# Expert feed-forward of a two-block convolution and expert model: units of 384 tokens, blocks of 512 columns, one unrolled order

## The reference

```python
def _L1_ffn_ref(x, Wm, bm, expert_emb, W1, b1, W2, b2, Wo, bo):
    h = x @ Wm + bm
    t = h.reshape(bs * L_ * H, HD)                 # 8 heads of 32
    w = jax.nn.softmax(t @ expert_emb, axis=-1)    # 16 experts
    topw, topi = jax.lax.top_k(w, 2)
    hmid = jax.nn.gelu(jnp.einsum('td,edi->tei', t, W1) + b1, approximate=False)   # 32 -> 128
    eo = jnp.einsum('tei,eio->teo', hmid, W2) + b2                                 # 128 -> 32
    sel = jnp.take_along_axis(eo, topi[:, :, None], axis=1)
    comb = (sel * topw[:, :, None]).sum(axis=1)
    return comb.reshape(bs, L_, d) @ Wo + bo       # added to the token
```

## Time and profile before

| what | value |
|---|---|
| time, median of 3 runs | 3064.53 us (3064.31 to 3074.47) |
| the profiled execution | 3055.83 us, its span 3054.1 us |
| PE busy | 2221.5 us, 73% of the span |
| DVE busy | 1406.6 us, 46% |
| ACT busy | 1319.1 us, 43% |
| POOL busy | 1021.1 us, 33% |
| the expert feed-forward | from about 1990 us to the end |

### The profile page before, as it was taken

One profiled execution on the slowest core, in us unless ns is written; L12 is line 12 of the kernel. 1 busy time (PEld: TensorE's weight loads), 2 busy tenths in 40 slices (PEclk: granted clock), 3 DMA queues, 4 the chain that ended last, 5 costly groups with the idle time before them and its releaser, 6 DMA issues. The chain is left out here.

```text
span 3054.1 us, 47716 instructions
## 1 busy us (share of the span) xinstructions
PE 2221.5 (73%) x13261; PEld 1209.0 (40%) x13262; DVE 1406.6 (46%) x2065; ACT 1319.1 (43%) x1759; POOL 1021.1 (33%) x796
## 2 busy tenths in 40 slices
PE   3999289999576740008755558489999999999998
PEld 1444155555343520006642225244444444444444
DVE  3565233333334566002225545456665556666553
ACT  1443111111133530002111114278788888888887
POOL 4332211110000001760027610056555555555554
PEclk7999657777687875559986669799999999999999
DMA  1010121110001633535542202265566565556554
GB/s 30 27 27 6 42 58 41 42 47 22 4 1 60 224 113 101 155 113 166 172 132 69 64 27 71 74 150 134 127 139 140 132 138 127 127 131 147 127 132 101
DMA packets 236895, 285.57 MB, mean 94 GB/s; under 512 B 29172, under 2 KB 218052, under 8 KB 236676
## 3 DMA queue, kind: packets, MB, share of 16 engines
q1 hardware_dynamic: 198116, 232.95, 31.0%
q0 software_dynamic: 12288, 25.72, 2.8%
q10 hardware_dynamic: 26400, 25.70, 2.4%
HBM read 209.00 MB, written 75.25 MB: 93 GB/s over the span
## 5 line engine op out<-in xcount | busy, mean ns | idle before, releaser
L2088 DVE SCALAR_TENSOR_TENSOR BIG<-psMO,b_s,BIG 128x392 f32<-128x392 f32 x512 | 315.1, 622 | 399.3 <-PE psMO L1971 395.2
L1958 POOL TENSOR_TENSOR BIG<-BIG 128x784 f32<-128x784 f32 x192 | 367.5, 1917 | 293.5 <-DVE BIG L2088 286.9
L2011 PE MATMUL ps<-x_r,w_r 128*128 128x392 f32 x1376 | 374.4, 372 | 0.7 <-ACT at L2047 0.5
L2047 ACT ACTIVATE xv<-ps,b_s 128x784 f32<-128x784 f32 x336 | 297.5, 911 | 52.7 <-PE ps L2011 51.9
L2011 PEld LDWEIGHTS ps<-x_r,w_r 128*128 128x128 f32 x1376 | 228.7, 189 | 210.1 <-issue 174.2
L1971 PE MATMUL psMO<-ex,w_s 128*32 128x392 f32 x512 | 213.1, 498 | 51.0 <-DVE BIG L2064 33.0
L1971 PE MATMUL psMO<-xv,w_s 128*32 128x392 f32 x2048 | 223.6, 507 | 23.3 <-issue 8.5
L1404 POOL DMA_INDIRECT gath<-yg_d,idx x128 | 133.6, 1044 | 268.3 <-DVE idx L1415 226.5
L1369 ACT ACTIVATE xv<-ps 128x512 f32<-128x512 f32 x66 | 39.4, 597 | 419.7 <-PE ps L1347 419.7
L1971 PE MATMUL psMO<-rz,w_s 128*32 128x392 f32 x512 | 216.3, 505 | 0.0
L1971 PE MATMUL psMO<-at,w_s 128*32 128x392 f32 x512 | 216.3, 505 | 0.0
(11 more groups left out here) (363 smaller groups left out, 4368.8 us busy)
## 6 DMA issues: line engine op xcount, KB each, us to landing
BIG<-wt_d SPq DMA_DIRECT2D x512, 196.0 KB, 4.1
BIG<-hs_d SPq DMA_DIRECT2D x128, 196.0 KB
xg_d<-zeros SPq DMA_DIRECT2D x64, 264.0 KB
xv<-xg_d SPq DMA_DIRECT2D x66, 256.0 KB, 3.1
BIG<-ypad_d SPq DMA_DIRECT2D x288, 56.0 KB
xv<-x SPq DMA_DIRECT2D x64, 196.0 KB, 3.5
yg_d<-ex ACTq DMA_DIRECT2D x33, 256.0 KB, 3.4
yg_d<-sq ACTq DMA_DIRECT2D x33, 256.0 KB, 3.4
```

Source lines behind the costliest of these rows:

```text
L1958: m = eng.tensor_tensor(dst, dst, src, ALU.add)
L2011: mm = eng.matmul(psA[bufs[m]][:, hh, 0:CH], w1_r[:, group * 4 + e], x_r[:, half, pair * 2 + hh], start=True, stop=True)
L2047: eng.activation(hid[m % 8], psA[bufs[m]][:, :, 0:CH], ACT.Gelu, bias=b1_s[:, ex_:ex_ + 1]).then_inc(Q["gel"], 1)
L2088: eng.scalar_tensor_tensor(out=gsum[:, it % 2, q], in0=psY[hh][:, 0:CH], scalar=b2_s[:, it % 4:it % 4 + 1], in1=wb[:, it % 2, q], op0=ALU. ...
```

## The change

Only the expert feed-forward changes, with the layout of the two device-memory arrays that feed it. The tokens are now cut into 16 pieces of 384 and a rest of 128. A piece is worked as two units `w` of four heads each, and the rest is one unit of eight heads, so that there are NU = 33 units. A unit is 1536 columns (the last 1024), which is three blocks of 512 (two). It has four groups of four experts, so there are 132 groups g.

A first product is now three matmuls of 512 columns with one weight into one of two PSUM buffers of three banks, and a gelu is 1536 columns long. A second product fills one of two banks with 512 columns, three times for a group. The two banks `psY` are now used strictly in turn by everything that needs one, with two counters, `put` (filled by PE) and `got` (emptied by DVE).

Everything is written out in 137 slots k with no loop. Slot k holds the four first products of group k and the second products of group k - 1 after the first product of experts 1, 2 and 3. An extra piece of work, if there is one, stands behind the first product of expert 0: the fold of unit w in slot 4w + 6, the output products of piece c in slots 8c + 11 and 8c + 12, the gate transposes of chunk r in slot 8r - 3. The copies of POOL are gone, since DVE writes the first group's results into `gacc` itself. The hidden tiles, `gacc` and `fin` lie in `BIG`, and the gates and `gsum` have buffers of their own. The router still works in chunks of 392.

```diff
-        NI, NP, NS = 8, 16, 64
+        NTOK = B * HW
+        UT = 384
+        BLK = 512
+        UNITS = [(UT * (w // 2), UT, 4 * (w % 2), 4) for w in range(2 * (NTOK // UT))]
+        UNITS.append((NTOK // UT * UT, NTOK % UT, 0, NH))
+        NU = len(UNITS)
+        NG = 4 * NU
+        NBLK = [n * heads // BLK for _, n, _, heads in UNITS]
+        PARTS = [(c * UT, min(UT, NTOK - c * UT)) for c in range(-(-NTOK // UT))]
         w1_s = BIG[:, 0:NE * HID].rearrange("p (e i) -> p e i", e=NE)
+        hid = BIG[:, 0:24 * BLK].rearrange("p (m c) -> p m c", m=8)
+        gacc = BIG[:, 24 * BLK:30 * BLK].rearrange("p (a c) -> p a c", a=2)
+        fin = BIG[:, 30 * BLK:30 * BLK + 2 * UT].rearrange("p (a c) -> p a c", a=2)
+        stk = xv[:].rearrange("p a u h c -> p (a u h c)")[:, 0:6 * BLK].rearrange("p (a c) -> p a c", a=2)
+        comb = ex[:].rearrange("p h c -> p (h c)")[:, 0:2 * UT].rearrange("p (a c) -> p a c", a=2)
...
+        x_r = sb("x_r", [128, 2, 3 * BLK], F32R)
+        wb = sb("wb", [128, 2, 3 * BLK])
+        gsum = sb("gsum", [128, 2, 3 * BLK])
...
-        psA, psY = (psN, psS, psZ), (psM, psO)
+        ps_ctx.close()
+        psA = [ctx.enter_context(nc.psum_tensor(f"psA{a}", [128, 3 * BLK], F32)) for a in range(2)]
+        psY = [ctx.enter_context(nc.psum_tensor(f"psY{a}", [128, BLK], F32)) for a in range(2)]
...
+        FOLD = {4 * w + 6: w for w in range(NU)}
+        LAST = {8 * c + 11 + m_: (c, m_) for c in range(len(PARTS) - 1) for m_ in range(2)}
+        LAST.update({4 * NU + 3 + m_: (len(PARTS) - 1, m_) for m_ in range(2)})
+        ROUTE = {8 * r - 3: r for r in range(1, T)}
+        SLOTS = 4 * NU + 5
...
+        EXTRA_USE, BLOCK_USE, uses = {}, {}, 1
+        for k in range(SLOTS):
+            if k in FOLD or k in LAST or k in ROUTE:
+                EXTRA_USE[k] = uses
+                uses += 1
+            for b in range(blocks_of(k - 1)):
+                BLOCK_USE[k - 1, b] = uses
+                uses += 1
...
+        def gates_load(eng, g):
+            wait(eng, Q["got"], done_group(g - 2))
+            tok, n, head, heads = UNITS[g // 4]
+            for e in range(4):
+                src = wt_d.ap()[:, tok:tok + n].rearrange("(h e) c -> e h c", h=NH)[g % 4 * 4 + e]
+                eng.dma_start(wb[32 * e:32 * e + 32, g % 2, 0:heads * n].rearrange("p (q c) -> p q c", q=heads),
+                              src[head:head + heads].partition_broadcast(32)).then_inc(q_wb[g % 2], 16)
...
+                heads_load(eng, 0)
+                gates_load(eng, 0)
+                for k in range(SLOTS):
+                    if k % 4 == 0 and k // 4 + 1 < NU:
+                        heads_load(eng, k // 4 + 1)
+                    if k % 8 == 0 and k // 8 + 1 < T:
+                        route_load(eng, k // 8 + 1)
+                    if k in ROUTE:
+                        route_store(eng, ROUTE[k], EXTRA_USE[k])
+                    if k + 1 < NG:
+                        wait(eng, q_wst, 16 * min((k + 1) // 8 + 1, T))
+                        gates_load(eng, k + 1)
...
-                        if P == 2:
-                            split(t, 1)
-                        if P == 10 and not is_last(t):
-                            split(t + 1, 0)
...
+                split(0)
+                for w in range(NU):
+                    n = BLK * NBLK[w]
+                    for g in range(1, 4):
+                        a = 3 * w + g - 1
+                        wait(eng, Q["got"], done_group(4 * w + g))
+                        wait(eng, Q["acc"], a)
+                        eng.tensor_tensor(gacc[:, w % 2, 0:n], gacc[:, w % 2, 0:n], gsum[:, a % 2, 0:n],
+                                          ALU.add).then_inc(Q["acc"], 1)
+                        if g == 1 and w + 1 < NU:
+                            split(w + 1)
...
+                def first(m):
+                    w = m // 16
+                    if m % 16 == 0:
+                        wait(eng, Q["lo"], w + 1)
+                    wait(eng, Q["gel"], m - 1)
+                    for b in range(NBLK[w]):
+                        mm = eng.matmul(psA[m % 2][:, b * BLK:(b + 1) * BLK], w1_r[:, m % 16],
+                                        x_r[:, w % 2, b * BLK:(b + 1) * BLK], start=True, stop=True)
+                    mm.then_inc(Q["mm1"], 1)
...
+                def second(g, b):
+                    use = BLOCK_USE[g, b]
+                    wait(eng, Q["gel"], 4 * g + 4)
+                    wait(eng, Q["got"], use - 1)
                     for e in range(4):
-                        mm = eng.matmul(psY[hh][32 * e:32 * e + 32, 0:CH], w2_s[:, (P // 2 % 4) * 4 + e],
-                                        hid[(P % 2) * 4 + e][:, hh], start=True, stop=True,
+                        mm = eng.matmul(psY[use % 2][32 * e:32 * e + 32, :], w2_s[:, g % 4 * 4 + e],
+                                        hid[:, (4 * g + e) % 8, b * BLK:(b + 1) * BLK], start=True, stop=True,
...
+                for k in range(SLOTS):
+                    for e in range(4):
+                        if k < NG:
+                            first(4 * k + e)
+                        if e == 0 and k in FOLD:
+                            fold(FOLD[k], EXTRA_USE[k])
+                        if e == 0 and k in LAST:
+                            last(*LAST[k], EXTRA_USE[k])
+                        if e == 0 and k in ROUTE:
+                            route_pe(eng, ROUTE[k], EXTRA_USE[k])
+                        if 0 < e <= blocks_of(k - 1):
+                            second(k - 1, e - 1)
...
+                for m in range(4 * NG):
+                    n = BLK * NBLK[m // 16]
+                    if m % 4 == 0:
+                        wait(eng, Q["put"], done_group(m // 4 - 2))
+                    wait(eng, Q["mm1"], m + 1)
+                    eng.activation(hid[:, m % 8, 0:n], psA[m % 2][:, 0:n], ACT.Gelu,
+                                   bias=b1_s[:, m % 16:m % 16 + 1]).then_inc(Q["gel"], 1)
...
+                for k in range(SLOTS):
+                    if k in FOLD:
+                        combine(FOLD[k], EXTRA_USE[k])
+                    if k in LAST:
+                        finish(*LAST[k], EXTRA_USE[k])
+                    if k in ROUTE:
+                        route_copy(eng, ROUTE[k], EXTRA_USE[k])
+                    r, i = k // 8 + 1, k % 8
+                    for b in range(blocks_of(k - 1)):
+                        weigh(k - 1, b)
+                        if r < T and i < 5:
+                            route(eng, r, (3 * i + b,))
+                    if r < T and i == 4:
+                        route(eng, r, (15,))```

On POOL, in the middle of the stage, the order of adds and splits changes. Before (the last chunk, where no loop hides it) the split stands behind the two copies of the first group and ahead of six adds:

```order
L1954 COPY BIG<-BIG 128x784 x2
L1933 CAST x_r<-BIG 128x1568
L1935 TENSOR_TENSOR x_r<-BIG,x_r 64x1568
L1958 TENSOR_TENSOR BIG<-BIG 128x784 x6
L1954 COPY BIG<-BIG 128x784 x2
L1958 TENSOR_TENSOR BIG<-BIG 128x784 x6
```

More of the change, by code:

```diff
@@ L1821, in chunks, with route_pe @@
-        def chunks(eng, body, tail):
-            body(0)
-            body(1)
-            with eng.Fori(2, T - 1) as t:
-                body(t)
-            body(T - 1)
-            tail(T)
-        def is_last(t):
-            return isinstance(t, int) and t == T - 1
+            eng.dma_start(rt[:, EXP].rearrange("p s e -> p (s e)"), ex_d.ap()[r]).then_inc(q_ex, 16)
+        def route_pe(eng, r, use):
+            wait(eng, Q["rt"], (r + 1) * RT2)
+            wait(eng, Q["got"], use - 1)
+            for s in range(NSUB):
+                m = eng.transpose(psY[use % 2][:, s * SUB:(s + 1) * SUB],
+                                  rt[:, M1, s * NH:(s + 1) * NH].rearrange("p h e -> p (h e)"), ident[0:SUB, 0:SUB])
+            m.then_inc(Q["put"], 1)
@@ L1984, in last, with fold @@
-                def last(t, m_):
-                    wait_alone(eng, Q["comb"], t * 2)
+                    mm.then_inc(Q["put"], 1)
+                def fold(w, use):
+                    tok, n, head, heads = UNITS[w]
+                    wait(eng, Q["acc"], 3 * w + 3)
+                    wait(eng, Q["got"], use - 1)
+                    for q in range(heads):
+                        mm = eng.matmul(psY[use % 2][q % 4 * 32:q % 4 * 32 + 32, q // 4 * n:(q // 4 + 1) * n], foldm[:],
+                                        gacc[:, w % 2, q * n:(q + 1) * n], start=True, stop=True,
+                                        tile_position=(0, q % 4 * 32))
+                    mm.then_inc(Q["put"], 1)
@@ L2094, in tail, with weigh @@
-                def tail(t):
-                    combine(t - 1, 1)
-                    for m_ in range(2):
-                        finish(t, m_)
-                chunks(eng, body, tail)
+                def weigh(g, b):
+                    use = BLOCK_USE[g, b]
+                    w = g // 4
+                    if b == 0:
```

(14 more changed lines are left out.)

266 lines of the change are left out of this document (75 added, 191 removed).

## The result

The changed kernel takes 3163.85 us (median of 5 runs, 3149.27 to 3170.91), the kernel before 3071.2 in the same comparison (5 runs). The ratio is 1.031, 95% interval 1.029 to 1.033: slower by 93 us. The forecast for the median was +55, so the direction, the range and the kind of loss were right. 3163.85 lies above the 3095 to 3145 that the forecast had for itself, in the stretch that it gave to the slower case with 0.22, and 38 us are to be accounted for. The profiled run of the changed kernel took 3149.27, the shortest of the five, with a span of 3147.5. It is 93.4 us over the profiled run before (3055.83), so the two traces differ by as much as the medians do.

The account below looks back on a forecast made before the run. PE was taken to bound the kernel. +3 us at full clock and +52 of clock losses on the profiled 3055.83 gave 3111, put at 3120 for the median of the runs; range 3050 to 3170.

Parts of the forecast that it names:

- the slower case: Rival: clock stays down past one slot or falls at every stand of slots 3, 5 and 7; 3163 us, chance 0.22.
- PE remains the bound: Plain slot of the feed-forward: PE needs 6.1 us, taken as 6.3 with waits; ACT at most 6.2.
- The split: Next unit's split behind group 1's add: 9.45 us in slot 7, 9.85 in slot 3; PE stands 3.15 and 2.2.
- The transposes: Slot 5: gate transposes wait for step 15, held up by POOL's add; PE stands 4.6 us, slot 11.25.
- the rival order: Slot 5: step 15 done ahead of POOL's add, 2.9 us shorter; 3025 us, chance 0.12 together with covered stands.
- The clock: PE's clock falls behind stands in slots 5, 7 (6 in 10) and 3 (2 in 10), 1.85 us each: 52 us.
- Loads change nothing: Gates are asked for over a slot ahead, same bytes, DMA busy 0.59 of the time: no cost.
- The prices of PE's pieces: PE, start to start: first product 0.77 us, second product 1.00, fold 0.66; eight slots sum to 64.7 at full clock.
- As meant: Rival: split and transposes find cover and the plain slot decides; about 2912 us, chance 0.12 together with the short step 15.

Follow-up runs that it names:

- The run with clock and load mended: The changed kernel with extra matmuls in all three stands of TensorE and the router's load issued two slots earlier: 3081.26 us, 1.008.
- the run with all three mended: The changed kernel with the router's load two slots earlier, the next unit's split ahead of the first add, gate transposes in slot 7: 2944.34 us, 0.9635.

## Why the prediction was right, and where it was short

- **PE remains the bound, nothing else replaces it.** Right. ACT's gelu takes 1542 ns (forecast 1.54), DVE's weighing 0.75 (0.75), POOL's add 3.50 (3.47), cast 1.48 (1.47), subtraction 3.43 (3.48). In slot 3, where a routing step of DVE runs beside it, the subtraction takes 3.78, which is the 0.4 that the forecast added there.
- **The split.** Right: 9.44 for 9.45 in slot 7 and 9.76 for 9.85 in slot 3, with stands of 2.94 and 2.04 us. With the split ahead of the add these two stands are gone, so its place is the cause.
- **The transposes.** Right: 3.79 for step 15, 4.41 for the stand, and the rival order is excluded, since step 15 took 3.79 in all 15 pairs and never slipped in ahead of the add. Taking the add out of its way, or the transposes out of slot 5, gives 82 to 87 us.
- **The clock.** Forecast 52 us, and 3.73 x 15.5 = 58 by the run that keeps PE at work. The total is near, the terms in it less so. Slot 5 lost the clock in all 15 pairs as forecast, at 2.1 each and not 1.85. Slot 7 lost it 15 times of 15, where the forecast had 6 in 10, at 1.4 each. In slot 3 the 3 of 14 agree with the forecast's 2 in 10, but that is luck: the same stand of 2.04 us lost the clock 4, 6, 8 and 14 times of 14 in the traces with the add held back, with PE kept at work ahead of the transposes, with the transposes in slot 7 and with the early load. The 3.7 us of low clock from which the price of 1.85 came stand in no row; the earlier trace rows have 3.1 us of it behind the start of the work. The Trainium skill, "TensorE: Matmul & The Clock Gate", section "HAM oscillation — how this bites in real kernels", describes a kernel in which the wait between bursts of matmuls throws the clock down every time, and that was nearer than my 6 in 10. The trace agrees for the stands of 2.9 and 4.4 us (15 of 15 each), and it does not carry over to those of 2.04.
- **"Loads change nothing": the step that failed.** It looked at the gates and at the DMA share and left out the router's load, whose new place is right behind eight other transfers and only 3 us ahead of the moment at which DVE could take it (2420.76 and 2424.03). It costs 0.68 us a pair as the changed kernel runs (slots 1 and 2 take 14.44 there and 13.77 with the early load), and 1.84 with the clock held. I had priced the loads by their bytes and by the gates' lead, and not each by its moment of issue.
- **The prices of PE's pieces, mis-sized.** The run with clock and load mended has 65.95 where the forecast had 64.7. Of these 1.25 us, 0.74 lie in the two fold slots and 0.15 in a plain one (6.44 for 6.3); slot 5 has 0.19 more, and slots 7 and 0 together 0.17. The reason shows in the starts of PE in the changed kernel:

```profile
2400.46 0.97 PE L1991 MATMUL psA<-x_r,w_r 128*128 128x512 f32 x3
2401.36 1.07 PE L2001 MATMUL psY<-BIG,w_s 128*32 128x512 f32 x8
2402.35 0.96 PE L1991 MATMUL psA<-x_r,w_r 128*128 128x512 f32 x3
2403.24 0.85 PE L2012 MATMUL psY<-BIG,fold 128*32 128x384 f32 x8
2404.03 0.97 PE L1991 MATMUL psA<-x_r,w_r 128*128 128x512 f32 x3
...
2409.70 1.68 PE L1991 MATMUL psA<-x_r,w_r 128*128 128x512 f32 x6
2411.30 1.07 PE L2001 MATMUL psY<-BIG,w_s 128*32 128x512 f32 x8
```

A first product alone takes 0.89 to the next start and two in a row 1.60, so 0.80 each. The forecast took half of a pair in a row and got 0.77. In the new order two first products stand side by side only in the three slots of eight that have no extra, so that 26 of 32 stand alone, and the fold, which also parts a pair, takes 0.79 itself and not the 0.66 of the earlier trace rows. The second product was right at 1.00. With these prices a fold slot is 4 x 0.89 + 3 x 1.00 + 0.79 = 7.35 (7.34 in the trace) and a plain one 2 x 0.89 + 1.60 + 3 x 1.00 = 6.38 (6.44).

Put together, a pair: 64.7 forecast, +1.25 prices, +0.68 late load, +3.73 clock = 70.36, against 70.35 in the trace. The terms are differences between columns of the table, so the sum has to close; what tests them is that the clock and the load were each taken away by a run of their own. The forecast's own clock term is 3.3 of the 3.73, so over 15.5 pairs the miss is some 19 us of prices, 10 of the load and 7 of the clock.

Of the rivals, the slower one (3163) gave the right time by another mechanism: its clock losses in all 47 places did not come, 33 did. "As meant" (2912, or 0.950 of its 3064.5) is not what the change does, but the run with all three mended has 0.9635. Its pair takes 57.25 where that rival's terms make 54.7. Of these 2.55 us, about half are the prices above, and 1.1 are short waits of PE for DVE (8.5 and 5.8 us in 13 pairs).

**What stays open.** Why the same stand of 2.04 us in slot 3 loses the clock 3 times of 14 in the changed kernel and 14 of 14 with the early load. PE has no idle 0.24 and 0.66 us ahead of it there. And with the early load all pairs from the second to the fifteenth are nearly of one length, 71.3 to 71.7 us, where in the changed kernel they vary from 69.0 to 71.8, so that each stand meets the clock in the same way or in a different one. No run separated the two, and each kernel has one trace. A stand a little under 3 us is not certain either: one of 2.92 us kept the clock in the trace with the add held back, and one in that with PE kept at work ahead of the transposes. Whether the router's load is slow because of the eight transfers ahead of it or would take 6.5 us in any case is open too, since the early load changes its place and its time at once, and so is why a first product costs 0.09 us more alone.

## What to carry to other kernels

When a change moves work in a written-out order, follow each small transfer to the moment of its issue: behind which waiting issue it stands and which engine takes it first. A DMA share of 0.59 says nothing of that. Losses on one path cover each other. Here the same late load was worth nothing by itself, 0.9% with the clock held, and 2.9% with the split and the transposes mended, so undo suspects together as well as singly before calling one harmless. And price a short matmul group in the neighbourhood in which it will stand, not where it is cheapest.

## What the runs showed of the hardware

- Useless matmuls in a stand of TensorE made the kernel 1.0 to 1.4% faster, because the granted clock stays at 1.00 in place of 0.50 for up to 5.5 us of work behind it. The stand itself does not get shorter.
- A stand of 2.04 us may or may not lose the clock, with the same length and the same work behind it (3, 4, 6, 8 and 14 of 14 in five kernels). Stands of 2.64 us lost it 10 times of 15. Those of 2.9 us lost it in every pair of the changed kernel and in 14 of 15 in two others, and those of 4.4 us every time.
- A GpSimd add of 3.8 us held up a VectorE step of 0.69 until 3.79. A wait added to GpSimd, so that the step goes first, gave 2.6%.
